# Gated slots on one Trainium2 core: half of two spreads issued on GpSimd's queue

## The reference, cut to what matters

```
q, k, v = silu(x Wq'), silu(x Wk'), silu(x Wv')
f = log_sigmoid(x Wf') / 8 ;  s = 1 - exp(f) ;  g = exp(f)
step 1:  S1 = S1 * g[None, :] + k[:, None] * s[None, :] ;  ok = q . S1
qv = softmax(ok)
step 2:  S2 = S2 * g[:, None] + s[:, None] * v[None, :] ;  ov = qv . S2
out = rmsnorm(silu(ov)) Wo'
```

## Time and profile before

| | |
|---|---|
| time, median of 3 runs | 4062.52 us (4061.97 to 4063.6) |
| the profiled execution's own time | 4065.85 us |
| its span | 4064.1 us |
| PE busy | 3490.2 us (86%) |
| DVE busy | 2725.7 us (67%) |
| ACT busy | 2282.9 us (56%) |
| POOL busy | 2063.6 us (51%) |
| DMAs issued by SP's kind of queue (q1) | 228.56 MB, 24.3% of 16 engines |
| DMAs issued by GpSimd (q0) | 17.97 MB, 1.4% of 16 engines |

### The profile page before, as it was taken

The page is one execution under the profiler, slowest core; times in us unless marked ns, Lnnn a source line. Parts: engine busy times, 40 slices in busy tenths (PEclk is TensorE's granted clock), DMA queues, the critical chain, the costliest instruction groups (busy, mean ns, idle before and its releaser), DMA issues. The chain is left out here.

```text
span 4064.1 us, 88951 instructions
## 1 busy us (share of the span) xinstructions
PE 3490.2 (86%) x30432; PEld 2159.0 (53%) x30527; DVE 2725.7 (67%) x7206; ACT 2282.9 (56%) x5536; POOL 2063.6 (51%) x2119
## 2 busy tenths in 40 slices
PE   5999999967767999999999999975947775987668
PEld 1333333316764656656566665665936664665446
DVE  6888888856445777777777777754456664655465
ACT  2777777744324666666666666642445552774367
POOL 3333333317435777777777677656421111665175
PEclk9999999985888999999999999966968887897879
DMA  5443343302561212112121221223632222110001
GB/s 101 61 60 60 60 60 60 60 21 65 172 191 42 51 44 53 47 49 51 44 53 46 49 50 45 53 63 106 204 81 65 64 64 48 30 58 5 1 1 43
DMA packets 418241, 252.23 MB, mean 62 GB/s; under 512 B 251186, under 2 KB 344354, under 8 KB 416642
## 3 DMA queue, kind: packets, MB, share of 16 engines
q1 hardware_dynamic: 409156, 228.56, 24.3%
q0 software_dynamic: 8640, 17.97, 1.4%
HBM read 75.12 MB, written 41.75 MB: 29 GB/s over the span
## 5 line engine op out<-in xcount | busy, mean ns | idle before, releaser
L2498 POOL TENSOR_TENSOR ra_prob<-ra_prob,ra_inverse 128x256 f32<-128x256 f32 (+3 forms) x512 | 631.3, 1254 | 367.4 <-DVE ra_inverse L2714 365.9
L2312 DVE TENSOR_REDUCE ca_mx<-ca_ps_s 128x2 f32<-128x1024 f32 x512 | 600.8, 1211 | 118.9 <-PE ca_ps_s L2184 118.6
L2643 ACT ACTIVATE ra_prob<-ra_ps_s,ra_low 128x128 f32<-128x128 f32 (+3 forms) x1024 | 534.5, 532 | 237.4 <-DVE ra_low L2694 237.4
L2249 ACT ACTIVATE ca_pT<-ca_ps_p 128x512 f32<-128x512 f32 x1024 | 544.8, 599 | 204.3 <-PE ca_ps_p L2194 179.9
L2694 DVE CUSTOM_DVE_ANT_0 ra_ps_s<-ra_ps_s,ra_mask 128x128 f32<-128x128 f32 (+3 forms) x1024 | 480.4, 511 | 47.0 <-PE ra_ps_s L2591 46.8
L2184 PE MATMUL ca_ps_s<-ca_kst,ca_qst 128*128 128x512 bf16 x991 | 380.4, 390 | 33.9 <-DVE ca_mx L2312 14.5
L2649 ACT COPY ra_probT<-ra_ps_t 128x512 f32<-128x512 f32 x384 | 227.3, 592 | 261.3 <-PE ra_ps_t L2537 261.3
L2194 PE MATMUL ca_ps_p<-ca_qst,ca_kst 128*128 128x512 bf16 x962 | 362.8, 382 | 6.2 <-ACT ca_pT L2249 4.8
L2537 PE MATMUL ra_ps_t<-ident,ra_prob 128*128 128x128 f32 x2560 | 350.2, 276 | 2.7 <-ACT ra_probT L2649 1.3
L2591 PE MATMUL ra_ps_s<-ra_kz,ra_qz 64*128 64x128 f32 (+3 forms) x2048 | 347.3, 458 | 3.7 <-DMA ra_kz<-ra_rot 2.8
L2491 POOL TENSOR_TENSOR ra_rot<-ra_prod 128x512 f32<-128x512 f32 x256 | 321.1, 1275 | 43.3 <-DVE ra_prod L2703 43.3
(11 more groups left out here) (411 smaller groups left out, 7177.7 us busy)
## 6 DMA issues: line engine op xcount, KB each, us to landing
moe_w_own<-moe_w1T SPq DMA_DIRECT2D x142, 256.0 KB
ra_qz<-ra_rot SPq DMA_DIRECT2D x512, 64.0 KB, 2.0
ra_kz<-ra_rot SPq DMA_DIRECT2D x512, 64.0 KB, 2.0
ca_kst<-ca_bounce SPq DMA_DIRECT2D x256, 64.0 KB
ca_bounce<-ca_thirds SPq DMA_DIRECT2D x192, 64.0 KB, 3.0
ca_qst<-ca_bounce SPq DMA_DIRECT2D x64, 192.0 KB
moe_hs<-moe_rows SPq DMA_DIRECT2D x142, 66.0 KB, 2.2
moe_raw<-in_L_ffn_W SPq DMA_DIRECT2D x32, 256.0 KB, 2.9
```

Source lines behind the costliest of these rows:

```text
L2249: nc.scalar.activation(pT[:, (NS * hp + u) % PRING, :], ps_p[n % NP][:], ACT.Exp).then_inc(sg["drained"], 1)
L2312: nc.vector.tensor_reduce(mx[:, hm % 2, 2 * j:2 * j + 2], ps_s[m % 2][:].rearrange("p (b k) -> p b k", b=2), AX.X, ALU.max)\
L2498: nc.gpsimd.tensor_tensor(at, at, inverse[:, n % PROB, 2 * tile:2 * tile + 2].unsqueeze(2).broadcast_to([P, 2, keys]), ALU.mult)\
L2643: nc.scalar.activation(prob[:, n % PROB, tile, head, 0:keys], part(n, tile)[:, head, :], ACT.Exp, bias=low[:, n % PROB, at:at + 1], scale= ...
```

## The change

SP's `spread` takes the groups to be sent. For `q2m` and `am2x` it sends groups 0 and 1 only. GpSimd sends groups 2 and 3 with a function of its own, `rest`, at the end of its step, after the same waits as SP, and with semaphores of their own (`q2m_rest`, `am2x_rest`). TensorE and VectorE wait for both halves.

```diff
-                def spread(out, rows, signal):
+                def spread(out, rows, signal, groups=range(4)):
 
-                    for j in range(4):
+                    for j in groups:
                         at = slice(j * BL, (j + 1) * BL)
                         sp.dma_start(out[at, j, :], rows[at, :]).then_inc(sg[signal], 16)
...
                         need(sp, "q2_done", i3)
                         need(sp, "o2_in", i4)
-                        spread(q2m[:], q2T[:], "q2m_landed")
+                        spread(q2m[:], q2T[:], "q2m_landed", range(2))
                         need(sp, "am2_done", i3)
-                        spread(masked(am2x[:]), am2[:], "am2x_landed")
+                        spread(masked(am2x[:]), am2[:], "am2x_landed", range(2))
...
-                        need(pe, "q2m_landed", i3, EXPAND)
+                        need(pe, "q2m_landed", i3, EXPAND // 2)
+                        need(pe, "q2m_rest", i3, EXPAND // 2)
...
-                        need(pe, "am2x_landed", i3, EXPAND)
+                        need(pe, "am2x_landed", i3, EXPAND // 2)
+                        need(pe, "am2x_rest", i3, EXPAND // 2)
...
                 pool.wait_ge(loaded, 128)
+                pool.wait_ge(zeroed, 4)
+
+                def rest(out, rows, signal):
+
+                    for j in (2, 3):
+                        at = slice(j * BL, (j + 1) * BL)
+                        pool.dma_start(out[at, j, :], rows[at, :]).then_inc(sg[signal], 16)
...
+                    if live(i3):
+                        need(pool, "q2_done", i3)
+                        need(pool, "o2_in", i4)
+                        rest(q2m[:], q2T[:], "q2m_rest")
+                        need(pool, "am2_done", i3)
+                        rest(am2x[:].rearrange("p j c h t -> p j (c h t)"), am2[:], "am2x_rest")
```

More of the change, by code:

```diff
@@ L1545, in gated_slots @@
                  "a2_in", "am2_done", "o2_in", "o_done", "osq_done", "ss_in", "ovar_done", "ors_done", "y_in", "added",
-                 "qm_landed", "kx_landed", "vx_landed", "am1x_landed", "q2m_landed", "am2x_landed")
+                 "qm_landed", "kx_landed", "vx_landed", "am1x_landed", "q2m_landed", "am2x_landed", "q2m_rest", "am2x_rest")
         sg = {n: sem(n) for n in names}
@@ L1916, in body @@
                         need(dve, "qv_turned", i3)
-                        need(dve, "q2m_landed", i4, EXPAND)
+                        need(dve, "q2m_landed", i4, EXPAND // 2)
+                        need(dve, "q2m_rest", i4, EXPAND // 2)
                         nc.vector.tensor_tensor(q2T[:], ps_t[:], eqT[:, i3 % 2], ALU.mult).then_inc(sg["q2_done"], 1)
@@ L1934, in body @@
                         need(dve, "a2_in", i3)
-                        need(dve, "am2x_landed", i4, EXPAND)
+                        need(dve, "am2x_landed", i4, EXPAND // 2)
+                        need(dve, "am2x_rest", i4, EXPAND // 2)
                         mask(am2[:], "am2_done")
```

## The result

The changed kernel took 4033.22 us (4023.99 to 4037.99, 4 runs), against 4062.24 us (4061.49 to 4063.6) for the kernel before on the same chip. The ratio is 0.9925, with an interval of 0.9907 to 0.9944: 29 us less. The forecast was 4057 us and its range began at 4035, so the change brought five times what the forecast gave it, and slightly more than the range allowed. The profiled execution took 4031.47 us, with a span of 4029.7.

The account below looks back on a forecast made before the run. TensorE, busy 74%, was taken to bound the kernel. Gains of 16 x 0.21 + 14 x 0.24 = 6.7 us, less about 1 us for waits, gave 4062.5 - 5.7 = 4056.8, say 4057 us; range 4035 to 4078.

Parts of the forecast that it names:

- the term t: One plain DMA issue on GpSimd, taken as 0.90 us; chain 1.90 + 2t, breaking even with 3.91 at t = 1.00.
- The other bound: Lower end for GpSimd's issue price: SP's 0.60 us for the same 32 rows, giving a chain of 3.10 us.
- Rival 1: GpSimd's plain issue costs about SP's 0.60 us: chain 3.10, kernel 4039 us; 4030 to 4050, chance 0.27.
- its variant without the gap: Issue at 0.60 us without the 0.30 between two on GpSimd: chain 2.80 us, kernel 4030 us.
- A second step: GpSimd's landing: 2.28 us from issue start, less 0.96 of issue, leaves 1.32 us behind the issue.
- the 0.21 of a typical step: Gain on TensorE's wait for `q2m`, chain 3.70 against 3.91 us, counted for 16 sequences.
- the work that hides GpSimd's issues: GpSimd idles 17.47 us before `osq`; issues are through some 5 us before it can start, so nothing is late.
- SP's later spreads: Spreads behind the divided ones on SP start 1.2 us earlier, costed at nothing.
- The two gains add: TensorE's waits for `q2m` and `am2x` each shrink by their own share, 0.21 and 0.24 us.
- The late partner behind a vanished first wait: ScalarE's results for the projections become due only if TensorE's first wait, 1.14 us, vanishes altogether.
- Rival 2: GpSimd's issue stretches beside VectorE to 1.23 us or more, slowing the kernel: 4065 to 4093 us, chance 0.23.
- Rival 3: The four DMAs share the same 16 engines and land no earlier: 4062 us, chance within the forecast case's 0.50.

Follow-up runs that it names:

- e4: Kernel before, with the second half of both spreads issued on ScalarE's queue and none on GpSimd: 4025.07 us, ratio 0.9914.
- e1: Kernel before, with only `q2m` divided between SP and GpSimd, `am2x` left on SP: 4038.01 us, ratio 0.995.
- e9: Changed kernel with GpSimd's half of `q2m` issued about 1 us later: 4047.4 us, ratio 0.9978 against the kernel before.
- e5: Changed kernel with one of GpSimd's two DMAs of each spread moved to ScalarE: 4025.97 us, ratio 0.9918 against before.

## Why the prediction was wrong

**The step that failed is the term t,** the price of one plain issue on GpSimd. I took 0.90 us, close to the indirect form "since the engine and the queue are the same", and kept its 0.30 between two issues. Measured are 0.50 to 0.55 us and no gap. The other bound, SP's 0.60 for the same 32 rows, was the right neighbour: like in the form of the instruction, not in the engine. Rival 1 had this mechanism, and its variant without the gap had the price nearly right. That this variant's 4030 us lies next to the 4033 measured is luck all the same: its chain of 2.80 did not come, and the late landings, worth some 8.5 us, were not in it.

**A second step failed the other way.** I counted 1.32 us from the end of the last issue to the landing, so that a shorter issue would also land sooner. Measured from the last issue's start, TensorE goes on after 3259.76 - 3257.44 = 2.32 us for `am2x`, and after 2.13 for `q2m`, against 2.28 in the prediction; from its end it is 1.83 and 1.63, not 1.32. So the start is the better base. With it the chain of `am2x` is 0.29 + 0.49 + 2.32 = 3.10, not rival 1's 2.80.

**The sum with both corrected** is 16 x 0.90 + 14 x 0.84 - 1 = 25 us, or 4037. The direction of the forecast and its structure were sound; its size was off by t. The measured time fell into the fastest end of rival 1, which the range had left out at a chance of 0.09.

**The late landings stood in the rows and I read past them.** The earlier trace rows says 31.3 us in 16 waits for `q2m`, 1.96 each, and the earlier trace rows shows 1.14. I multiplied the 0.21 of a typical step by 16. The difference of the mean from the typical was the eight late sequences, worth 22.9 - 16 x 0.90 = 8.5 us more than the shortened chain gives, if all the rest were equal.

**What came back.** The other idle times grew by 7.5 us: 2.5 of it is a wait for VectorE's `qv`, and 5.0 lie inside `before`, where no row names a cause. The 10.1 us of shorter matmuls I did not count at all. The pause of 4.05 us behind the layer I did not foresee either: I named the work that hides GpSimd's issues, and looked at no work behind the layer.

**What was right.** The issues stand behind a wait on VectorE and hold up no `osq`: its row is idle for 5.53 us ahead of it and is ended by ScalarE, not by a DMA. SP's later spreads cost nothing and gained nothing that a row shows. The two gains add inside the layer (25.2 + 8.7 against 34.8, one execution each). The late partner behind a vanished first wait is ScalarE (e4). Rival 2 falls, since the issues run at 0.50 to 0.65 beside VectorE's adds and scans. What it said of the earlier trace rows, that the issue did not wait for the end of the scalings, does not follow: the row of 1.11 us is four operations of 0.34 to 0.43 each, and a growth of 0.27 fits into one of them. Rival 3 falls with e1 and e9, since a list that starts its last DMA earlier lands earlier.

The Trainium skill, DMA: Bandwidth & Descriptors, section "Issuing engines are not separate DMA queues", says that several issuing engines save only the time of issuing, which is usually small beside the transfer. The trace agrees with the first half. The second half doesn't hold for a list of four such DMAs: 1.8 of the chain's 3.9 us are issue.

## What to carry to other kernels

A list of small DMAs that an engine waits for is worth dividing over two issuing engines, and a plain issue costs about the same on each of them (here 0.50 to 0.55 us on GpSimd, 0.57 to 0.60 on SP, 0.71 on ScalarE), so price it by a plain issue and not by another form on the same engine. When the mean of a wait is far from what a typical step shows, look for the few long ones before multiplying. And a DMA on GpSimd has a bill at the end of the layer here (4.05 us for 64), which ScalarE's queue does not have: 34 us gained instead of 29, though the intervals overlap.

## What the runs showed of the hardware

- A plain DMA costs GpSimd 0.49 to 0.55 us of issue for 32 or 128 rows of 512 B or 2 KB; the indirect form into off-chip memory 0.96 with 0.30 between two. TensorE goes on 2.1 to 2.3 us behind the start of the last issue in the changed kernel.
- At the end of the layer each plain DMA that GpSimd has issued in it costs 0.082 us of pause (32, 64, 92 and 128 DMAs: 3.82, 6.44, 8.76 and 11.67 us behind its last operation). What GpSimd does in that time, no row shows.
- A copy between on-chip tiles on VectorE stretched four issues on GpSimd by 1.23 us, and the two issues beside a copy ended 0.1 us behind it; additions with two on-chip inputs did not.
- One packet of the `instruction` queue, some 0.9 to 1.6 us long, goes with a spread that lands 0.8 to 1.8 us late, in 26 of 27 sequences where it starts 2.4 to 3.5 us behind `q2T` and the spread is to land at 3.7 us or later.
- TensorE's granted clock in the layer was 0.88 before and 0.92 after, and the same matmuls took 10.1 us less. It did not follow the waits in all runs: 0.93 in e9 with 79 us idle in the stretch, 0.91 in e5 with 61.
